# An up-projection issued one step later on TensorE, in a state-space convolution with a gated low-rank FFN

## What is computed

```
# cond: masked long convolution of each head
mask = arange(L) < length[:, None];  u_m = u * mask
K = 2 * einsum('hn,hnl->hl', C * (exp(dtA) - 1) / A, exp(dtA[:, :, None] * arange(L))).real
y = irfft(rfft(u_m, 2L) * rfft(K, 2L))[..., :L] + u_m * D[:, None];  y = y * mask
# ffn: top-1 routed low-rank projection, over the last axis
logits = einsum('bsd,ed->bse', y, route_w);  topk_v, topk_idx = top_k(logits, 1)
wh = (one_hot(topk_idx) * topk_v)[..., None] * einsum('bsd,erd->bser', y, A)
out = x + einsum('bser,eor->bso', wh, Bw)
```

## Time and profile before

| | us |
|---|---|
| median of 3 runs (lowest to highest) | 646.25 (645.07 to 647.22) |
| the profiled execution, timed | 645.36 |
| span of the profiled execution | 643.5 |
| TensorE busy | 602.9 (94%) |
| VectorE busy | 514.0 (80%) |
| ScalarE busy | 376.6 (59%) |
| GpSimd busy | 370.0 (57%) |

### The profile page before, as it was taken

How to read it: one execution, slowest core, us unless ns; L and a number is a source line. 1 busy time by engine, 2 the same in 40 slices (tenths; PEclk the granted TensorE clock), 3 DMA queues, 4 the chain that set the end, 5 groups by cost and what they waited for, 6 DMA issues and landing times.

```text
span 643.5 us, 13947 instructions
## 1 busy us (share of the span) xinstructions
PE 602.9 (94%) x3681; PEld 531.6 (83%) x3681; DVE 514.0 (80%) x1436; ACT 376.6 (59%) x1164; POOL 370.0 (57%) x474
## 2 busy tenths in 40 slices
PE   3489999999999999999999999999999999999996
PEld 2378888888888888888888888888888888888884
DVE  7788887878788787878878887887888778788775
ACT  3675665565566566556656655665665566566430
POOL 4466656655755665575566557556655755665530
PEclk9999999999999999999999999999999999999999
DMA  6023453344445345434534543443454454344422
GB/s 139 11 84 90 133 148 103 128 141 129 106 135 149 95 133 143 120 112 140 147 93 134 145 114 117 141 144 95 134 146 111 120 141 141 95 137 145 109 83 98
DMA packets 37074, 77.68 MB, mean 121 GB/s; under 512 B 11836, under 2 KB 20350, under 8 KB 36998
## 3 DMA queue, kind: packets, MB, share of 16 engines
q1 hardware_dynamic: 27846, 43.76, 29.1%
q10 hardware_dynamic: 9152, 33.03, 12.6%
HBM read 43.16 MB, written 33.62 MB: 119 GB/s over the span
## 4 chain that ended last, share of the span: by engine, by line
PE 89%; DVE 4%; issue 4%; POOL 2%; ACT 0%; DMA 0%; POOLq 0%; ACTq 0%
PE psYo L988 18%; PE psZ L1011 18%; PE psO L988 16%; PE psYe L988 12%; PE psS L988 10%; PE psO L1037 4%; PE psXe L1001 4%; PE psXo L1001 4%; PE psZ L1076 1%; PE psZ L1049 1%; POOL Grev L436 0%; DVE brought L853 0%; DMA logs<-in_L_cond_log_dt_dram 0%; POOL wave L426 0%; DVE ex L694 0%
## 5 line engine op out<-in xcount | busy, mean ns | idle before, releaser
L468 POOL TENSOR_TENSOR Slo<-Sf,Shi 128x384 fp32r<-128x384 f32 x64 | 65.2, 1020 | 236.8 <-ACT Shi L591 236.8
L1011 PE MATMUL psZ<-Wt,Y 128*128 128x136 f32 x1024 | 129.1, 279 | 0.0
L1011 PEld LDWEIGHTS psZ<-Wt,Y 128*128 128x128 f32 x1024 | 126.9, 190 | 0.4 <-DVE Y L876 0.3
L853 DVE SCALAR_TENSOR_TENSOR brought<-Sf,tab,psS 64x128 f32<-64x128 f32 x256 | 89.0, 348 | 36.2 <-ACT Sf L586 29.8
L885 DVE TENSOR_TENSOR ost<-psO,xt 128x512 f32<-128x512 f32 x128 | 81.9, 676 | 1.1 <-PE psO L988 1.1
L461 POOL TENSOR_TENSOR Xlo<-xeven,Xhi 128x512 fp32r<-128x512 f32 x64 | 82.6, 1291 | 0.0
L531 ACT ACTIVATE Ghi<-Grev 128x256 fp32r<-128x256 f32 x64 | 26.7, 417 | 78.6 <-POOL Grev L436 78.6
L869 DVE TENSOR_TENSOR wlo<-psZ,whi 128x128 fp32r<-128x128 f32 x64 | 18.6, 291 | 67.2 <-ACT whi L596 67.2
L586 ACT ACTIVATE Sf<-psS 128x128 f32<-128x128 f32 x64 | 17.7, 277 | 93.1 <-PE psS L988 93.1
L988 PE MATMUL psO<-Bw_hi,whi 128*128 128x512 f32 x128 | 55.1, 430 | 12.1 <-issue 11.0
L569 ACT ACTIVATE Xhi<-psXe 128x512 fp32r<-128x512 f32 x64 | 38.2, 596 | 37.4 <-PE psXe L1001 37.4
(11 more groups left out here) (194 smaller groups left out, 1691.5 us busy)
## 6 DMA issues: line engine op xcount, KB each, us to landing
xt<-in_x_dram SPq DMA_DIRECT2D x64, 512.0 KB, 4.2
out_dram<-ost ACTq DMA_DIRECT2D x63, 512.0 KB, 5.1
Traw<-kdram SPq DMA_DIRECT2D x64, 128.0 KB, 2.9
kdram<-krow SPq DMA_DIRECT2D x64, 1.0 KB
A_nat<-in_L_ffn_A_dram SPq DMA_DIRECT2D x1, 512.0 KB, 4.9
B_nat<-in_L_ffn_Bw_dram SPq DMA_DIRECT2D x8, 64.0 KB, 3.6
out_dram<-ost SPq DMA_DIRECT2D x2, 256.0 KB, 2.0
lens_i<-in_itok_B_dram SPq DMA_DIRECT2D x1, 64.0 KB, 3.8
```

What stands on the lines that cost most here:

```text
L468: pool.tensor_tensor(Slo[h.s2][:, :], Sf[h.s2][:, :], Shi[h.s2][:, :].bitcast(F32), ALU.subtract).then_inc(slo_done, 1)
L853: dve.scalar_tensor_tensor(brought[to, :], Sf[h.s2][fr, old], tab2[fr, BR, h.n:h.n + 1], psS[to, new], ALU.mult, ALU.add).then_inc(brought ...
L1011: last = pe.matmul(psZ[:, 0:NW], Y[:, j, c, :], Wt[:, 2 * c + j, :], start=(j == 0 and c == 0), stop=(j == 1 and c == NE - 1), skip_group_ ...
```

## The change

Four things are changed, all in the order in which engines issue; no instruction is added or taken away.

- TensorE: `up` no longer stands at the end of the step for head i - 1 but behind `bring`, for head i - 2. It waits for the tables of head i + 1 instead of i + 2 in `psO[0]`, the same head seen from its new place.
- VectorE: the two adds go with it, from the end of the step (head i - 1) to behind `carry` (head i - 2). `whole_turns` goes from ahead of the cuts to the start of the next step, ahead of `carry`.
- ScalarE: `s_hi` is issued ahead of the two `x_hi` instead of behind them, `w_hi` ahead of `t_hi`, and the store is that of head i - 3 instead of i - 2.
- GpSimd: `turn_parts` is written at the start of the next step instead of the end of this one, which gives the same sequence. All steps run once more (66 instead of 65), so that the last head's up-projection, adds and store are reached.

```diff
--- before.py
+++ after.py
@@ -279,7 +279,7 @@
                 eng.wait_ge(s, count)
 
         def run_steps(step):
-            for i in range(H + 1):
+            for i in range(H + 2):
                 step(lambda d, i=i: Head(i + d))
 
         def col(t, h):
@@ -469,6 +469,8 @@
                                    ALU.subtract).then_inc(slo_done, 1)
 
             def step(head):
+                if head(3).there and not is_head(head(0), 0):
+                    turn_parts(head(3))
                 if head(0).there and not is_head(head(0), 0):
                     s_lo(head(0))
                 if head(1).there:
@@ -479,8 +481,6 @@
                     t_lo(head(1))
                 if head(3).there:
                     g_lo(head(3))
-                if head(4).there:
-                    turn_parts(head(4))
 
             first = [Head(n) for n in range(4)]
             turn_parts(first[0])
@@ -602,14 +602,13 @@
                     turns(head(4))
                 if head(3).there:
                     m_matrix(head(3))
-                if head(-2).there:
-                    store(head(-2))
+                if head(-3).there:
+                    store(head(-3))
+                if head(0).there and not is_head(head(0), 0):
+                    s_hi(head(0))
                 if head(1).there and not is_head(head(0), 0):
                     x_hi(head(1), 0)
                     x_hi(head(1), 1)
-                if head(0).there and not is_head(head(0), 0):
-                    s_hi(head(0))
-                if head(1).there and not is_head(head(0), 0):
                     x_even(head(1))
                 if head(2).there:
                     b_hi(head(2))
@@ -617,10 +616,10 @@
                     sines(head(3))
                 if head(2).there:
                     k_row(head(2))
+                if head(-1).there:
+                    w_hi(head(-1))
                 if head(1).there:
                     t_hi(head(1))
-                if head(-1).there:
-                    w_hi(head(-1))
                 if head(3).there:
                     g_hi(head(3))
 
@@ -886,11 +885,16 @@
                                   ALU.add).then_inc(added, 1)
 
             def step(head):
+                if head(3).there and not is_head(head(0), 0):
+                    whole_turns(head(3))
                 if head(0).there:
                     carry(head(0))
                 if is_head(head(0), 0):
                     whole_turns(head(3))
                     x_lo(head(1))
+                if head(-2).there:
+                    add(head(-2), 0)
+                    add(head(-2), 1)
                 if head(-1).there:
                     largest(head(-1))
                 if head(3).there:
@@ -909,14 +913,9 @@
                     b_lo(head(2))
                 if head(-1).there:
                     w_lo(head(-1))
-                if head(4).there:
-                    whole_turns(head(4))
                 if head(0).there:
                     cut(head(0), 0)
                     cut(head(0), 1)
-                if head(-1).there:
-                    add(head(-1), 0)
-                    add(head(-1), 1)
 
             first = [Head(n) for n in range(4)]
 
@@ -1092,6 +1091,8 @@
             def step(head):
                 if head(0).there:
                     bring(head(0))
+                if head(-2).there:
+                    up(head(-2), head(1))
                 if head(-1).there:
                     project(head(-1), 0)
                     project(head(-1), 1)
@@ -1111,8 +1112,6 @@
                     turn_wh(head(-1))
                 if head(0).there:
                     from_states(head(0))
-                if head(-1).there:
-                    up(head(-1), head(2))
 
             def turn_tables(pack, bank_, n):
                 for t in range(n):
```

## The result

| | us |
|---|---|
| changed kernel, median of 5 runs (lowest to highest) | 642.29 (639.73 to 642.93) |
| kernel before, median of 5 runs (lowest to highest) | 645.71 (645.07 to 647.22) |
| ratio, 95% interval | 0.9933 (0.9908 to 0.9958) |
| profiled execution of the changed kernel, timed, and its span | 639.73, 637.9 |

The change gained 0.7%, some 3.4 us. The prediction had 620.6 us, within 617 to 632, and so missed by 22 us: the sign came out, the size by no means.

A forecast was written before the change was run, and what follows sets the result against it. TensorE's work plus its wait ahead of `up` was taken as the bound; removing 61 x 0.42 = 25.6 us, with start and end net zero, gave 646.25 - 25.6 = 620.6 us, forecast 617 to 624, 8-in-10 range to 632.

The forecast's parts named there:

- The sign: Whole kernel: faster by over 0.3% given 0.87, same 0.05, slower 0.08.
- What bounds the kernel, and what goes.: TensorE's wait ahead of `up`, ended by `wlo`: 0.42 us a step goes, 61 times; step 9.40 to 8.98 us.
- Start and end: First steps lose 0.7 us (bounds 0 and 2), step 63 regains about as much, last store 0 to 0.5; net zero.
- the queues: Load of `xt`, write of `kdram` and the store: each costs zero, with more than 3 us of cover.
- `bring`: Next `bring` at 8.98 us wants GpSimd's `Xlo`, which ends at 7.81: 1.17 us of cover.
- the first add: On VectorE, ends at about 4.64 us; `inputs` needs its bank at 5.17, a cover of 0.5 us.
- the paragraph on VectorE: `whole` delays the carry 0.1 us, to 3.92; adds follow, `gate` starts at 6.25, `turn_wh` has 0.9 us cover.
- The margin: `gate` at 6.25 us starts ahead of GpSimd's `Xlo` at 6.53; over 0.28 us later, it would collide.
- The slower rival: `gate` falls behind GpSimd's `Xlo`, steps take 9.5 to 9.55 us, 654 us in all; chance 0.08.
- The recovery: After a late `gate`, TensorE is late, `Glo` finishes before `whole`, the next carry is early and the step recovers.
- my second rival: Half the gain: `inputs` waits for the first add, or `gate` is late one step in three; 633 us; chance 0.09.
- The hold of VectorE by GpSimd: Port rule: `Slo` delayed `gate` 0.68 us; `frac` given 0.09; `gate` at 6.45 instead of 6.25 would move no term.

## Why the prediction was wrong

- **The sign** is right, but by less than it looks. With 29 late steps instead of 21 the time was 646.43 us, no gain at all; that the collision came less often than in every second step was not forecast.
- **What bounds the kernel, and what goes.** Right. The wait ahead of `up` was 0.42 us a step, ended by `wlo`, and it is gone; a step without collision takes 9.00 us, against 8.98 worked out. With the collision removed the kernel measured 620.0 us, against the sum's 620.6.
- **Start and end, the queues, `bring`, the first add.** Right as a sum. The span with `gate` from PSUM is 617.9 us, 643.5 - 25.6. Of the 25.6 us the 58 steady steps gave 23.8, the start 1.6 and the end 0.35: the steady step gained a little less than worked out, and the start a little more, which is luck. No wait at `bring` or on a DMA has appeared in the steady steps, and none at `inputs` but with `Shi` moved back.
- **The step that failed** is the paragraph on VectorE, the term "I give the carry 0.1 us for it". `whole` starts at 1.05 as worked out, but `Glo`, for which the prediction worked out no start, begins at 0.94 to 1.00, just ahead of it, and lasts some 0.73 us. So in 35 of the 36 steps with a small margin `whole` takes 0.77 to 0.84 us instead of the 0.28 that it needs alone, and the carry ends 0.3 us late, at 4.12 to 4.19, and not 0.1 us late at 3.92. The 0.1 had no row behind it, though the earlier trace rows gave the means to work it out. `frac` took 0.61 us, of which 0.13 was waiting, not 0.09. With both, `gate` came at 6.48 to 6.56 instead of 6.25.
- **The margin.** Worked out as 0.28 us, with the point of decision at 0. `Xlo` came at 6.60, 0.07 later than worked out, and so the margin was 0.04 to 0.12 us in 36 of the 58 steps. And the decision does not lie at 0 but at 0.10 us: `gate` was held in 21 of the 36. That the earlier trace rows showed 0.25 us as harmless said nothing on 0.1.
- **The slower rival** was the right mechanism, with the right place, and 0.08 was too little for it: the margin of 0.28 us rested on a chain of instructions of which two could be held, each hold put at 0.1 us. Its price was too low. A late step costs 0.91 us and not 0.55, since `turn_k`, which stands ahead of `turn_wh`, waits for the same `wh`, TensorE begins 0.25 us behind the end of `wh` (311.44 to 311.69), and reaches `from_states` 0.32 us after that in the step shown (312.01), where a good step has 0.14. In full, with every step late, it gives 674.6 us, not 654.
- **The recovery** was described, and used as an argument against the rival. It is real, though `Glo` does not finish ahead of `whole`, as the prediction had it; it only starts earlier. It makes the collision occur in every second or third step instead of in all. I did not draw the conclusion that a collision that is cured for one step comes back in the next, in other words that the likely outcome was a mixture, of the kind that "`gate` is late in one step of three" describes in my second rival. That place had the time at 633 us with the low price, and with the measured price 639.
- **The hold of VectorE by GpSimd** was seen in the earlier trace rows, and I took it for what moves no term of the sum. It moved the one that mattered: `whole` and `Glo`, beside each other at 1.04, meet in every step. And the `gate` at 6.45 that the prediction worked out as the later case would have left a margin of 0.08 us, on the wrong side.

## What to carry to other kernels

When a schedule is laid out from rows and an engine pair can hold each other, work out every hold on the way to the critical instruction, and not only its own. A margin of 0.27 us and more held in all steps here, one of 0.1 us did not. Price the collision in full, with everything that stands in the queue behind it, and expect it in a share of the steps if a late step restores the margin. A small VectorE instruction on the critical chain that can meet GpSimd is best put in a form that needs only one SBUF input, the other from PSUM, if its operand lies there anyway: it was worth 22 us here, and nothing in the kernel before, where it met nothing. An engine whose busy time rises without more instructions is waiting inside them; the list of waits does not show that, the minimum, median and maximum of one tile do.

## What the runs showed of the hardware

- A VectorE instruction held by GpSimd is recorded as longer, not as a wait. It ends before its own time would allow if it started at GpSimd's end: `gate` ended at 311.12, 0.03 us after `Xlo` (311.09), though it needs 0.29 alone, so that it got in some 0.26 us earlier; `frac` some 0.20 us ahead of the end of `Slo`, `whole` some 0.12 us ahead of that of `Glo`.
- The order of the start times in the records does not settle who is held. The Trainium skill, SBUF — State Buffer, section Who interferes with whom, lets whoever issues first have the port; the records show starts and not issues, and here a `gate` recorded 0.05 us first was held for 1.1 us, and one recorded 0.11 us first was not. The border for this `tensor_scalar` was 0.102 us in three traces; the form with two SBUF inputs was still free at 0.086. Where in an instruction the port is taken was not measured.
- Nor did `Xlo`, as the second to start beside a `gate` that got in, wait for its end: it began 0.11 us behind it and took 1.34 us (300.80 above) instead of 1.30, where waiting for `gate` to end would have cost 0.18. Small as they are, a late step followed in all 40 cases in the three traces.
